# One accumulator bank for products and sums, a ring of 16 probability tiles, and two groups of tiles summed by VectorE along a stride

## What is computed

```python
def _L0_conv_ref(x, mask, Wq, bq, Wk, bk, Wv, bv, Wf, bf):
    m = jax.image.resize(mask, (B, 1, H, W), method='bilinear')
    q = proj(Wq, bq) / math.sqrt(hd)
    k = proj(Wk, bk)
    v = proj(Wv, bv)
    attn = jax.nn.softmax(jnp.einsum('bnd,bmd->bnm', q, k), axis=-1)
    fuse = jnp.einsum('bnm,bmd->bnd', attn, v)
    fuse = fuse.transpose(0, 2, 1).reshape(B, C, H, W)
    hybrid = _conv1x1(jnp.concatenate([x, fuse], axis=1), Wf, bf)
    return hybrid * m + x * (1.0 - m)

def _L1_conv_ref(x, ...):
    edge = jax.nn.relu(bn(dwconv3x3(x, edge_w), ...))
    att = jax.nn.sigmoid(jax.nn.relu(mean(x) @ fc1_w.T) @ fc2_w.T)
    out = conv1x1([x * att, edge], fusion_w) + fusion_b
    out = bn(conv1x1(dwconv3x3(bn(out), deform_w), balance_w) + balance_b)
    return out * x
```

## Time and profile before

| | |
|---|---|
| time, median of 3 runs (lowest to highest) | 4200.41 us (4199.91 to 4203.75) |
| the profiled execution, its own time | 4203.13 us |
| its span | 4201.3 us |
| busy in the span: PE, DVE, POOL, ACT | 96%, 84%, 77%, 56% |
| scores run from, to | 296.1, 3736.0 us |
| projection phase ends, about | 227 us |
| image phase begins, about | 3762 us |

### The profile page before, as it was taken

How to read it: one execution, slowest core, us unless ns; L and a number is a source line. 1 busy time by engine, 2 the same in 40 slices (tenths; PEclk the granted TensorE clock), 3 DMA queues, 4 the chain that set the end, 5 groups by cost and what they waited for, 6 DMA issues and landing times. The chain is left out here.

```text
span 4201.3 us, 81722 instructions
## 1 busy us (share of the span) xinstructions
PE 4044.0 (96%) x20341; PEld 1975.3 (47%) x20341; DVE 3550.1 (84%) x5350; ACT 2339.9 (56%) x4424; POOL 3222.2 (77%) x1360
## 2 busy tenths in 40 slices
PE   7979999999999999999999999999999999969797
PEld 4534444444444444444444444444444444424343
DVE  3279999999989999999899999999999999917989
ACT  1216666666656666666566666666666666641213
POOL 2429999999989999999899999999999999960000
PEclk9959999999999999999999999999999999989998
DMA  6931100110001101110111011100110000013021
GB/s 190 285 100 39 41 21 22 42 39 22 21 23 41 31 21 32 41 31 21 31 41 31 21 31 38 35 20 18 40 38 21 21 21 21 17 27 85 20 80 40
DMA packets 213798, 184.92 MB, mean 44 GB/s; under 512 B 115986, under 2 KB 140740, under 8 KB 213316
## 3 DMA queue, kind: packets, MB, share of 16 engines
q1 hardware_dynamic: 213508, 181.74, 16.2%
HBM read 122.10 MB, written 59.24 MB: 43 GB/s over the span
## 5 line engine op out<-in xcount | busy, mean ns | idle before, releaser
L761 ACT ACTIVATE prob<-st 128x512 f32<-128x512 f32 x4096 | 2154.3, 601 | 1309.3 <-PE st L626 1048.6
L819 DVE TENSOR_REDUCE block_max<-mx 128x1 f32<-128x512 f32 x4096 | 2562.0, 683 | 343.4 <-PE mx L633 330.0
L490 POOL TENSOR_TENSOR prob_sum<-prob_sum,prob 128x1024 f32<-128x1024 f32 x768 | 1929.3, 2512 | 127.5 <-POOL prob_sum L490 100.4
L633 PE MATMUL mx<-keys,max_queries 96*128 96x512 f32 x4096 | 1648.0, 426 | 38.2 <-DMA keys<-k_scratch 27.8
L626 PE MATMUL st<-queries,keys 97*128 97x512 f32 x4096 | 1574.5, 411 | 1.6 <-ACT prob L761 1.5
L490 POOL TENSOR_TENSOR prob_sum<-prob 128x1024 f32<-128x1024 f32 x448 | 1067.8, 2383 | 253.1 <-ACT prob L761 253.1
L633 PEld LDWEIGHTS mx<-keys,max_queries 96*128 96x128 f32 x4096 | 777.8, 191 | 737.3 <-DVE block_max L819 564.8
L645 PE MATMUL acc<-prob,values 128*32 128x512 f32 x8192 | 1039.7, 602 | 0.0
L626 PEld LDWEIGHTS st<-queries,keys 97*128 97x128 f32 x4096 | 776.7, 190 | 520.6 <-ACT prob L761 282.2
L645 PEld LDWEIGHTS acc<-prob,values 128*32 128x32 f32 x8192 | 194.4, 108 | 427.1 <-issue 226.1
L665 PE MATMUL dacc<-prob_sum,ones 128*32 128x512 f32 x2048 | 273.0, 605 | 9.2 <-POOL prob_sum L490 9.2
(11 more groups left out here) (119 smaller groups left out, 1213.8 us busy)
## 6 DMA issues: line engine op xcount, KB each, us to landing
max_queries<-q_scratch SPq DMA_DIRECT2D x384, 64.0 KB, 1.9
queries<-q_scratch SPq DMA_DIRECT2D x384, 64.0 KB, 2.0
keys<-k_scratch SPq DMA_DIRECT2D x168, 128.0 KB, 2.5
x<-in_x SPq DMA_DIRECT2D x18, 512.0 KB, 4.1
q_scratch<-high SPq DMA_DIRECT2D x32, 256.0 KB, 4.4
k_scratch<-high SPq DMA_DIRECT2D x16, 512.0 KB, 4.9
q_scratch<-low SPq DMA_DIRECT2D x32, 256.0 KB, 5.0
k_scratch<-low SPq DMA_DIRECT2D x16, 512.0 KB, 4.9
```

Of the source, the lines that this page charges most:

```text
L490: ops.tensor_tensor(psum[k][:, :, :], a[:, :, :], prob[(first + i) % RING][:, :, :], ALU.add).then_inc(added[own], 1)
L633: nc.tensor.matmul(mx[bank(j, p)][:, :], qm[p][:, h, ns * P:(ns + 1) * P], kk[gp][0:SPLIT, h, blk * CH:(blk + 1) * CH], start=True, stop=T ...
L761: nc.scalar.activation(prob[s % RING][:, h, :], st[bank(i, p)][:, :], ACT.Exp).then_inc(exp_done, 1)
L819: nc.vector.tensor_reduce(bmax[p][:, j // MB, j % MB:j % MB + 1], mx[bank(j, p)][:, :], AX.X, ALU.max).then_inc(mx_taken, 1)
```

## The change

- **Groups.** All 32 tiles are in 8 groups of four; there are no plain tiles and 4 S instead of 5. VectorE has groups 2 and 5, GpSimd 18 additions instead of 19, taken in an order (`chain_order`) that puts the first addition of the next chain ahead of the last of this one.
- **VectorE's additions** become reductions. `prob` is one tensor with the ring as an axis; a group of four tiles is summed in one instruction for each head and half of the columns (`add_up`, 4 pieces a group, 256 columns each). The innermost axis of the read steps over the four tiles, 4 KiB apart.
- **Banks.** Products and sums take turns in the one bank `acc`. ScalarE copies both halves of the products (`num_part`) and later the whole bank of sums (`den`, 128 partitions); the halves of the sums are added in column layout. The freed bank becomes a fourth `mx`.
- **Ring and order.** The ring has 16 tiles for 8. `ORDER` is another, with its places for VectorE and ScalarE; scores run 27 ahead (13 before), maxima 40 (29 before).
- **Room.** The ring takes the room of the image phase's weights (`wf`, `fu`, `ba`, `diag`, 1.66 MB in all). They are stored to HBM in the projection phase and loaded again at the start of the image phase, which also makes the first mask there, ahead of `mixer`; TensorE's first mix waits for all of it.

```diff
-GROUPS = [4, 4, 4, 4, 3, 3, 4, 4]
-BY_VECTOR = [3]
+GROUPS = [4, 4, 4, 4, 4, 4, 4, 4]
+BY_VECTOR = [2, 5]
...
-RING = 8
+RING = 16
-ORDER = ("msmsmsVmsmsmsmsVsmsmsmsmsmVmsmsmsmsmsVVVsmsmsmssmsmsmsVVsmmsmssSVsmssmmsVV"
-         "mssmsmmssmsmSmssmsmmVmssmsmmVmsmssmmVmmsmssmSmsmsmsmVmssmsmmVSsmsmsmsSsmsms")
-SCORES_AHEAD = 13
-BLOCKS_AHEAD = 29
-TAKE_NUM, TAKE_DEN, INVERT = 24, 32, 40
-ADD_AFTER = [43, 51, 54]
-NUM_AFTER, DEN_AFTER = 6, 13
-SCALE_AFTER = 4
+ORDER = ("msmsmsmsmsmsVVVsmsmsmssmmsmssmsmsmsmVVsmssmmsmsmsmsVVVsmssmmsmmsVVVVVmsmss"
+         "mmmsmsVmmsmmsmsVmsmsmsmsmsmsmsmVssmmsSsmsmsmsmsmmssmsmSmsmssmmsmsmsSSsmsms")
+SCORES_AHEAD = 27
+BLOCKS_AHEAD = 40
+TAKE_NUM, INVERT = 22, 58
+ADD_AFTER = [36, 45, 45, 55, 58, 62, 62, 62]
+NUM_AFTER, DEN_AFTER = 6, 23
+SCALE_AFTER = 10
...
+def chain_order():
+    chains = [k for k, size in enumerate(GROUPS) if k not in BY_VECTOR and size > 1]
+    order = [(k, i) for k in chains for i in range(1, GROUPS[k])]
+    for k, after in zip(chains, chains[1:]):
+        if GROUPS[k] > 2:
+            order.remove((after, 1))
+            order.insert(order.index((k, GROUPS[k] - 1)), (after, 1))
+    return order
+PIECES = [(k, h, half) for k in BY_VECTOR for h in range(2) for half in range(2)]
...
-        prob = [sb(f"prob{r}", [P, 2, CH]) for r in range(RING)]
+        prob = sb("prob", [P, RING, 2, CH])
...
+        def add_up(dve, u, k, h, half):
+            first, last = GROUP_END[k] - GROUPS[k], GROUP_END[k] - 1
+            dve.wait_ge(sums_done, SUMS * u + k // 2 + 1)
+            dve.wait_ge(exp_done, TILES * (u + 1) + 2 * last + h + 1)
+            cols = slice(half * CH // 2, (half + 1) * CH // 2)
+            tiles = prob[:, first % RING:last % RING + 1, h, cols].rearrange("p t n -> p n t")
+            nc.vector.tensor_reduce(psum[k][:, h, cols], tiles, AX.X, ALU.add).then_inc(added[True], 1)
...
             def values(u, gp, q):
                 if q == 0:
-                    pe.wait_ge(num_ready, u + 1)
+                    pe.wait_ge(den_ready, u + 1)
...
             def sums(u, i):
                 if i == 0:
-                    pe.wait_ge(den_ready, u + 1)
+                    pe.wait_ge(num_out, 2 * (u + 1))
...
-                nc.scalar.copy(num_even[:, :], acc[0:2 * HD, :]).then_inc(num_half, 1)
+                for a in range(2):
+                    nc.scalar.copy(num_part[a][:, :], acc[2 * HD * a:2 * HD * (a + 1), :]).then_inc(num_out, 1)
...
-                nc.scalar.copy(den_even[:, :], dacc[0:2 * HD, :]).then_inc(den_half, 1)
+                nc.scalar.copy(den[:, :], acc[:, :]).then_inc(den_ready, 1)
...
-                nc.vector.tensor_tensor(num[:, :], acc[2 * HD:4 * HD, :], num_even[:, :], ALU.add).then_inc(num_ready, 1)
+                nc.vector.tensor_tensor(num[:, :], num_part[0][:, :], num_part[1][:, :], ALU.add).then_inc(num_ready, 1)
...
+            sp.dma_start(flat(late["wf"]), scratch["wf"][:, :]).then_inc(weights_back, 16)
+            load(0, 0, 0)
+            load_mask(0)
+            load(0, 1, 1)
+            for w in IMAGE_WEIGHTS[1:]:
+                sp.dma_start(flat(late[w]), scratch[w][:, :]).then_inc(weights_back, 16)
...
+            pe.wait_ge(weights_back, 16 * len(IMAGE_WEIGHTS))
             pe.wait_ge(mixer, CT)
...
-            dve.sem_inc(mstep, NM)
+            dve.wait_ge(mask_loaded, 16)
+            upsample(nc, dve, small, mask, mstep, 0)
             for t in range(CT):
                 own = keep["wf"][:, t, t * P:(t + 1) * P]
                 nc.vector.tensor_tensor(own, own, keep["ident"][:, :], ALU.subtract).then_inc(mixer, 1)
```

More of the change, by code:

```diff
@@ L272, in _ @@
             load(0, 1, 1)
-            sp.dma_start(small[0][:, :, :].rearrange("p h w -> p (h w)"),
-                         dram["mask"].rearrange("b a h w -> (b a) (h w)")[0:1, :].broadcast_to((P, 1024))
-                         ).then_inc(mask_loaded, 16)
+            for w in IMAGE_WEIGHTS:
+                sp.dma_start(scratch[w][:, :], flat(keep[w])).then_inc(put_away, 16)
             with sp.Fori(0, B) as b:
@@ L350, in _ @@
                         ins.then_inc(v_copied, 1)
-            dve.wait_ge(mask_loaded, 16)
-            upsample(nc, dve, small, keep["mask"], mstep, 0)
-            dve.wait_ge(mstep, NM)
         @block.gpsimd
@@ L427, in attention_phase @@
         warm = sb("exp_warm", [P, 1])
-        num_even = sb("num_even", [2 * HD, CH])
-        den_even = sb("den_even", [2 * HD, CH])
+        num_part = [sb(f"num_part{a}", [2 * HD, CH]) for a in range(2)]
         num = sb("num", [2 * HD, CH])
-        den = sb("den", [2 * HD, CH])
-        dcol = sb("den_col", [P, 2 * CH // P])
+        den = sb("den", [P, CH])
+        dcol = sb("den_col", [P, 2, 2 * CH // P])
+        dsum = sb("den_sum", [P, 2 * CH // P])
         rcol = sb("rec_col", [P, 2 * CH // P])
@@ L660, in sums @@
                     pe.wait_ge(exp_done, TILES * (u + 1) + 2 * t + 4)
-                    src = [prob[(t + a) % RING] for a in range(2)]
+                    src = [prob[:, (t + a) % RING, :, :] for a in range(2)]
                 for a in range(2):
@@ L850, in unit @@
             def unit(u, prev=True):
-                for k, size in enumerate(GROUPS):
-                    if k not in BY_VECTOR:
-                        for i in range(1, size):
-                            add(pool, nc.gpsimd, u, k, i)
-                    if k == SCALE_AFTER and prev:
+                for n, (k, i) in enumerate(CHAINS):
+                    add(pool, u, k, i)
+                    if n == SCALE_AFTER and prev:
                         scale(u - 1)
@@ L880, in image_phase @@
         xf = [sb(f"xf{p}", [P, 2 * CT, CH]) for p in range(2)]
-        mask = keep["mask"]
+        mask = sb("mask", [P, HH, WW])
+        late = image_weights(sb)
+        keep = {**keep, **late}
         small = [sb("m32", [P, 32, 32]), sb("q32", [P, 32, 32]), sb("m64", [P, 32, WW])]
@@ L950, in _ @@
         def _(sp):
-            sp.sem_inc(mask_loaded, 16)
             for p in range(2):
@@ L996, in image @@
                 store(b, NCH // 2, NCH)
-            for p in range(2):
-                load(0, p, p)
+            sp.dma_start(flat(late["wf"]), scratch["wf"][:, :]).then_inc(weights_back, 16)
[4 more added lines that the diff above has]
+                sp.dma_start(flat(late[w]), scratch[w][:, :]).then_inc(weights_back, 16)
             for p in range(2):
@@ L1294, in _, with image_weights @@
             image(B - 1, False)
+def image_weights(sb):
+    late = {w: sb(f"{w}T", [P, kts, ots * P]) for w, ots, kts in WEIGHTS if w in IMAGE_WEIGHTS}
+    late["diag"] = sb("diag", [P, CT, EDGE_PE, P])
+    return late
 def build(nc, dram, out):
@@ L1329, in build @@
         with ExitStack() as first:
-            weights = {w: first.enter_context(nc.sbuf_tensor(f"{w}T", [P, kts, ots * P], F32))
-                       for w, ots, kts in WEIGHTS if w in PROJECTIONS}
+            early = lambda name, shape: first.enter_context(nc.sbuf_tensor(f"first_{name}", shape, F32))
+            weights = {w: early(f"{w}T", [P, kts, ots * P]) for w, ots, kts in WEIGHTS if w not in IMAGE_WEIGHTS}
+            weights.update(image_weights(early))
             setup_phase(nc, dram, {**keep, **weights})
```

123 lines of the change are left out of this document (61 added, 62 removed).

## The result

4486.24 us, median of 4 runs (4481.26 to 4493.43), against 4201.07 for the kernel before beside it: ratio 1.0679 (95% interval 1.0661 to 1.0698). 4080 was forecast, with 4010 to 4230 as its range; it became slower by 6.8%, as rival C had it. The profiled execution took 4481.26 us, its span is 4479.5.

What follows compares the result with a forecast made beforehand. TensorE was taken as the bound, with VectorE level after the change. 62 units at -2.15 us, -6 for the tail, +3 projection and +15 image phase gave -121 us: from the 4200.4 median to 4080 us, range 4010 to 4230.

Steps and rivals of the forecast that it cites:

- rival C: VectorE's strided read is slow: a piece of 1.6 to 2.3 us, 4310 to 4655 us in all; chance 0.20.
- the price of a piece: VectorE's reduction of 1024 elements to 256 over four tiles: 1.22 us alone, 1.14 in a queue, eight a unit.
- Both bounds: For one VectorE piece: 1.22 us (1.14 in a queue) at full rate, 2.4 us (2.3) at the slow reading.
- 0.9 of coupling: Time a unit takes above its bounding engine's work, 0.9 us before the change, added again to the new unit.
- its unit: Steady attention unit: both engines near 50.5 us plus 0.9, so 51.5 us, 2.15 less than before.
- No piece waits for GpSimd: VectorE's reductions have one SBUF input, so no wait charged; waiting as additions do would cost 8 x 1.1 us more.
- TensorE's wait at S0: In the shared bank, S0 waits for ScalarE to copy both halves of the products: about 0.3 us a unit.
- TensorE's gap before the first mix: Start of the image phase: mask made before the mixer and weights reloaded, 15 us later, upper bound 20.
- `num` waits: On VectorE, `num` now reads two SBUF tiles and waits 0 to 2.4 us for GpSimd; 1.1 taken.
- The projection phase: 1.66 MB of weights stored and a 0.5 MB load gone: 4.0 us at most, 3 taken.
- The prologue's first interval: Start of attention: 11 more maxima and 14 more scores ahead, given back by unit 1's earlier maximum: 0.
- The tail of attention: End of attention, GpSimd's chain shorter by an addition and the start ahead: -6 us (0 to -12).

## Why the prediction was wrong

**The step that failed** is the price of a piece: "I take the lower end", 1.14 us in a queue. It is 1.94. Both bounds were written down, the true value lay between them, and the rows could not choose. The reasons that I gave for the lower end were about the write (every second element, once per group), and the read is what costs. The copy of 32 elements in 203 ns was the row that bore on it; rival C read it as running in pairs of slow streams. By the 1.67 ns measured for a far word, 30 elements more would add 50 ns as one stream and 25 as two; the rows show 33, nearer to two, so that reading was the better one (argued, not shown: that copy also writes with hops, of 256 bytes, and its read was never timed alone). The 220 ns for 64 elements, which the prediction puts down to the earlier trace rows, stand in the earlier trace rows; they are of a dense read. The right lesson of 1.14 against 2.3 with no row between was a larger chance for C than 0.20.

**Rival C** gave 4310 to 4655, deciding at a piece of 1.38 us; 4486 lies inside. Its sum by the measured piece is 4200.4 + 62 x (55.9 + 0.9 - 53.64) + 12 = 4408, which falls 78 us short: its 0.9 of coupling was not there, and the 128 us above 56.0 a unit, most of them the clock's, are a term that no rival had. So that 4486 lies in C's range is half luck: the unit came as C's sum has it, the rest is a second effect. The Trainium skill (Vector Engine (DVE) Microarchitecture Reference, section 5.2) gave 1.73 ns per column where one of two sources hops each time, and 4430 by it; the trace agrees nearly, with 1.81 ns for each element here (1.67 alone). The same section saw full rate where a single stream alternates between two far regions; L99 above agrees (512 results in 1222 ns), but four words are not two. What the same section states of runs of two adjacent words I had left out; it would have told that the hop is free in another layout, not that this one is fast.

**What held.** With the pieces at full rate the kernel takes 4086 us for the 4080 forecast, and its unit 51.8 on the mean for 51.5. No piece waits for GpSimd (L109; 1959 to 2065 ns in all 512). TensorE's wait at S0 is not to be seen in the steady units. TensorE's gap before the first mix grew by 15.9 us for 15 forecast.

**Smaller misses.** `num` waits in no steady unit (0.67 us; I had 1.1 more). The projection phase cost nothing: the first negated maximum came 2.7 us earlier, for +3. The prologue's first interval is 9.7 longer in the changed kernel, 4.7 with adjacent words (61.82), for 0. The tail of attention, which is the 13.5 less 15.9, gave 2.4, for 6.

**Not settled.** How much of the kernel with spread pieces is waits and how much clock; for which engine the instruction packets at VectorE's loop return are; and why one wait brings the clock down and another of the same length does not. In the changed kernel 1.26 and 0.61 us were followed by a fall and 1.25 and 0.23 were not, and with group 5 alone and the one-input sum 27 of 60 waits of about 1.0 us were.

## What to carry to other kernels

Price a reduction by where its successive reads lie, not by its element count: if the layout can put pairs side by side, a strided sum costs what a dense one does. When a change brings two engines level, a miss in the price of the one is paid twice, by its own length and by TensorE's clock, which falls behind the waits; so leave the engine that TensorE waits for some slack, or keep the load that it had. And give no VectorE instruction two SBUF inputs beside a gapless GpSimd queue, however small it is.
